# An LSTM with a rank-8 adapter: the adapter's weight generator read in 1 MB transfers of outer dimension 8

## The chip, the cores and the metric

The kernel runs on one core of a Trainium2 chip. Its metric is the device time of one execution in microseconds: 602.32 as the median of three runs before the change (600.86 to 602.75). One further execution was profiled; all rows below are from it.

## What is computed

`x` is 16 sequences of 256 tokens with 256 features, float32. First an LSTM runs over the tokens and its output is added to `x`. Then an adapter works on the result: a two-layer network of `cond` generates, for each of the 16 sequences, four weight quarters of rank 8, which act beside two shared 256 x 256 matrices.

```python
xz = einsum('ntd,dk->ntk', x, Wx) + b
def step(carry, xz_t):
    prev_h, prev_c = carry
    ai, af, ao, ag = split(xz_t + prev_h @ Wh, 4, axis=1)
    next_c = sigmoid(af) * prev_c + sigmoid(ai) * tanh(ag)
    next_h = sigmoid(ao) * tanh(next_c)
    return (next_h, next_c), next_h
x = x + lstm(x)

c = layernorm(cond) * gamma + beta
h = gelu(c @ W1 + bias1)                  # 16 x 256
w = h @ W2 + bias2                        # W2 is 256 x 8192, 8 MB
a1, b1, a2, b2 = split(w, 4), each (16, 256, 8)
u   = einsum('btd,bdr->btr', x, a2)
mid = gelu(x @ base_down + einsum('btr,blr->btl', u, b2))
v   = einsum('blr,btl->btr', b1, mid)
out = x + mid @ base_up.T + einsum('bkr,btr->btk', a1, v)
```

## The kernel before

The 256 tokens are 256 dependent steps, in 32 blocks of 8. All instructions are written out; the five engines run their own lists and meet at semaphores.

One step, on the critical path: TensorE multiplies the last hidden state with `Wh` into two banks `z` and one `z_o` (L712; 64 and 32 records of small matmuls), VectorE transposes the gates (L868, L872), ScalarE takes tanh (L422, L428, L434), VectorE forms the cell and the new `h_t` (L878 to L893). The banks are seeded beforehand by ScalarE with the projected input of the step (L358, L362).

Everything else of a block is laid into the steps. In step s of block k, TensorE transposes the `x` of block k+3 (L483), projects block k+2 with `wx` in eight pieces (L502, table `PIECES`), and does the adapter of block k-1 (L515 to L558). VectorE evacuates the projection into `proj` (L802). Then SP copies `proj` into `seed`, four transfers of 16 partitions each (L255), because the steps want it in another layout; ScalarE waits for this in step 7 of the block before, in front of that step's own second tanh (L439).

The weights of the adapter are made in the first blocks. In block 0 TensorE transposes the normed `cond` (step 2), multiplies it with `W1` (step 3, L607) and ScalarE makes `hid` from it. From step 11 on (`W_FIRST`) each step takes one of 16 portions of W2 (L633): four quarters of four portions, so the quarters begin in steps 11, 15, 19 and 23, counted from 0. Three SBUF tiles hold the quarters; the fourth goes into the first's tile.

SP issues all loads from one list, in order. A W2 portion is read in two transfers of 256 KB, 64 partitions each (L282). Each waits until the transfer three before it has landed (`UNDER_WAY`), so at most three are in flight. Between them SP issues the other loads of the block: `x` (L244), four of `w_bias` (L289, 16 partitions each) and the seeds. A wait of SP holds up all that stands behind it in the list.

Of the kernel before, what the change touches and what calls it, by code (L numbers as in the profile page):

```python
# [21 lines left out]
ACT = mybir.ActivationFunctionType  # L22
# [4 lines left out]
P = 128  # L27
NQ, NM, C = 4, 2, 32
# [11 lines left out]
LN_EPS = 1e-5  # L40
QUARTERS = (2, 1, 3, 0)
W_FIRST = 11
UNDER_WAY = 3
W_COLS = D * RANK // NQ
W_HALF = W_COLS // 2

# [3 lines left out]

N_PIECES = 8
PIECES = ((0, 0, 0, 2, 2, 4, 5, 7, 8), (0, 1, 2, 3, 4, 5, 6, 7, 8), (0, 1, 2, 3, 4, 5, 6, 7, 8))
EVACUATE_AT = (1, 3, 5, 7)
N_X = 4
WARM_UP = 6
# [2 lines left out]
def lstm_adapter(nc, x, cond, Wx, Wh, b, base_up, base_down, gamma, beta, W1, bias1, W2, bias2, out):  # L59
    ctx = ExitStack()  # L60
    with ctx:
# [6 lines left out]
        def sem(name):  # L68
# [26 lines left out]
        c_norm = sb("c_norm", [B, D])  # L95
        c_stat = sb("c_stat", [B, 5])
        c_t = sb("c_t", [P, 2, B])
        w1 = sb("w1", [P, 2, D])
        b1_col = sb("b1_col", [P, 2])
        hid = sb("hid", [P, 2, B])  # L100
        w2_tiles = [sb(f"w2_{n}", [P, 2, D * RANK]) for n in range(3)]
# [44 lines left out]
        zeroed = sem("zeroed")  # L146
        w_loaded = {n: sem(f"{n}_loaded") for n in
                    ("wx_g", "wx_if", "wx_o", "wh_g", "wh_if", "wh_o", "b", "down", "up", "ln", "cond", "w1")}
        w2_loaded = [[[sem(f"w2_loaded{q}_{i}_{r}") for r in range(2)] for i in range(NQ)] for q in range(4)]
        w_bias_zeroed, w_bias_loaded = sem("w_bias_zeroed"), sem("w_bias_loaded")  # L150
        w_placed = [sem(f"w_placed{q}") for q in range(4)]
        wx_ready, wh_ready = sem("wx_ready"), sem("wh_ready")
# [85 lines left out]
        @block.sync  # L238
        def _(sp):
            def load_x(f):  # L240
                first = f.k * TB
                if f.at_least(2):
                    sp.wait_ge(xt_psum, f.k - 1)
                sp.dma_start(x_nat[f.par][:, :], x[:, first:first + TB, :]).then_inc(x_loaded[f.par], 16)  # L244

            def load_seed(f):
                consumed = f.k * TB - TB
                if f.at_least(2):
                    for gone in (*seeded, seeded_o):
                        sp.wait_ge(gone, consumed)  # L250
                else:
                    sp.wait_ge(seeds_zeroed, f.k + 1)
                for j in range(NQ):
                    sp.wait_ge(xz_ready, f.k * XQ + (j + 1))
                    sp.dma_start(seed[f.par][32 * j:32 * j + B, :, :], proj[f.par][:, ZW * j:ZW * (j + 1)])\  # L255
                      .then_inc(seed_loaded[f.par], 16)

            def store_y(a):
                first = a.blk.k * TB
                sp.wait_ge(y_copied[a.lane], a.seq.k + 1)  # L260
                sp.dma_start(out[:, first:first + TB, :], y_nat[a.lane][a.seq.par][:, :])\
                  .then_inc(stored[a.lane][a.seq.par], 16)

            by_half = "(m p) n -> p m n"

            def load_cols(dst, src, lo, src_lo, n, name):
                sp.dma_start(dst[:, :, lo:lo + n], src.rearrange(by_half, m=NM)[:, :, src_lo:src_lo + n])\
                  .then_inc(w_loaded[name], 16)

            w2_parts = W2.rearrange("(k p) (q j h n) -> q h k p j n", p=P, q=4, j=NQ, n=W_HALF)  # L270

            def load_w2(piece):

                n, i = divmod(piece, NQ)
                q, (h, kc) = QUARTERS[n], divmod(i, 2)
                if piece == 3 * NQ:
                    sp.wait_ge(w_psum, 2)
                for r, rows in enumerate((slice(0, P // 2), slice(P // 2, P))):
                    back, half = divmod(2 * piece + r - UNDER_WAY, 2)
                    if back >= 0:  # L280
                        sp.wait_ge(w2_loaded[QUARTERS[back // NQ]][back % NQ][half], 16)
                    sp.dma_start(w2[q][rows, kc, :].rearrange("p (j h n) -> p h j n", j=NQ, n=W_HALF)[:, h],  # L282
                                 w2_parts[q, h, kc, rows]).then_inc(w2_loaded[q][i][r], 16)

            bias_q = bias2.rearrange("(q j n) -> j q n", q=4, j=NQ)

            def load_w_bias(j):
                sp.wait_ge(w_bias_zeroed, 1)
                sp.dma_start(w_bias[32 * j:32 * j + B, :, :], bias_q[j].partition_broadcast(B)).then_inc(w_bias_loaded, 16)  # L289

            load_x(Blk(0, 0))
            load_cols(wx, Wx, 2 * H, 3 * H, H, "wx_g")
            load_cols(wx, Wx, 0, 0, 2 * H, "wx_if")
            load_cols(wx, Wx, 3 * H, 2 * H, H, "wx_o")
            load_cols(wh, Wh, 2 * H, 3 * H, H, "wh_g")
            load_cols(wh, Wh, 0, 0, 2 * H, "wh_if")
            load_cols(wh, Wh, 3 * H, 2 * H, H, "wh_o")
            load_x(Blk(0, 1))
            sp.dma_start(c_gamma[:, :], gamma.partition_broadcast(B)).then_inc(w_loaded["ln"], 16)
            sp.dma_start(c_beta[:, :], beta.partition_broadcast(B)).then_inc(w_loaded["ln"], 16)  # L300
            load_seed(Blk(0, 0))
            load_x(Blk(0, 0, 2))
            sp.dma_start(w1[:, :, :], W1.rearrange("(k p) n -> p k n", p=P)).then_inc(w_loaded["w1"], 16)
            sp.dma_start(b1_col[:, :], bias1.rearrange("(k p) -> p k", p=P),
                         allow_slow_non_contiguous=True).then_inc(w_loaded["w1"], 16)
            load_cols(up_raw, base_up, 0, 0, D, "up")
            load_seed(Blk(0, 1))
            load_cols(down, base_down, 0, 0, D, "down")

            def one_block(k, front):  # L310
                if not k.at_least(1):
                    load_w2(0)
                    load_w2(1)
                if k.plus(3).exists():
                    load_x(k.plus(3))
                for piece in {0: range(2, 8), 1: range(8, 13), 2: range(13, 4 * NQ)}.get(k.k, ()):
                    load_w2(piece)
                    if 2 <= piece < 2 + NQ:
                        load_w_bias(piece - 2)
                if front:  # L320
                    load_seed(k.plus(2))
                done = follower(k.plus(-1))
                if done and done.seq.exists():
                    store_y(done)
                if early(k):
                    store_y(early(k))

            schedule(one_block)
            store_y(follower(Blk(NBLK // 2 - 1, 1)))
            for m in both:  # L330
                sp.wait_ge(tail_copied[m], 1)
# [7 lines left out]
        def _(act):  # L339
# [39 lines left out]

            def make_weights(k, s):  # L380

                if k == 0 and s == 3:

                    act.wait_ge(w_loaded["w1"], 32)
                    act.wait_ge(hidden_psum, 1)
                    for i in range(2):
                        act.activation(hid[:, i, :], aux[:, i * B:(i + 1) * B], ACT.Gelu,
# [25 lines left out]
            def one_block(k, front):  # L413
                a, e, done = follower(k), early(k), follower(k.plus(-1))
                for s in range(TB):
# [31 lines left out]
                        act.wait_ge(ht_ready[1], n + 1)  # L447
                        seed_o(ahead.par, s_next)

                    if s == 1 and not k.at_least(1):  # L450
                        evacuate_x(k.plus(2))
                    if not k.at_least(EARLY + 2):
                        make_weights(k.k, s)
# [24 lines left out]
        def _(pe):  # L478
# [115 lines left out]
            def make_weights(k, s):  # L594
# [5 lines left out]
                        ins = pe.transpose(aux[:, i * B:(i + 1) * B], c_norm[:, i * P:(i + 1) * P], ident[0:B, 0:B])  # L600
                    ins.then_inc(cond_t_psum, 1)
                if k == 0 and s == 3:
                    pe.wait_ge(w_loaded["w1"], 32)
                    pe.wait_ge(cond_t_ready, 1)
                    for i in range(2):
                        for kc in range(2):
                            ins = pe.matmul(aux[:, i * B:(i + 1) * B], w1[:, kc, i * P:(i + 1) * P], c_t[:, kc, :],  # L607
                                            start=(kc == 0), stop=(kc == 1))
                    ins.then_inc(hidden_psum, 1)
                if k == 0 and s in (4, 5):  # L610
# [8 lines left out]
                if 0 <= k * TB + s - W_FIRST < 4 * NQ:  # L619
# [6 lines left out]
                        pe.wait_ge(up_ready, 2)  # L626
                    elif kc == 0:
                        pe.wait_ge(w_biased, 2 * n + h)
                    for half in w2_loaded[q][i]:
                        pe.wait_ge(half, 16)  # L630
                    for j in range(NQ):
                        first = W_COLS * j + W_HALF * h
                        ins = pe.matmul(out_bank[32 * j:32 * j + B, 0:W_HALF], hid[:, kc, :],  # L633
# [38 lines left out]
                ins.then_inc(b_psum, 1)  # L672
            project(Blk(0, 0), range(N_PIECES))
            transpose_x(Blk(0, 1), both)
            project(Blk(0, 1), range(6))

            pe.wait_ge(w_loaded["wh_if"], 16)
            pe.wait_ge(w_loaded["wh_o"], 16)
# [2 lines left out]
            def one_block(k, front):  # L681
# [3 lines left out]
                for s in range(TB):  # L685
# [65 lines left out]
                    if front:  # L751
                        if not k.at_least(1):
                            if s == 0:
                                project(Blk(0, 1), range(6, N_PIECES))
                            if s == 1:
                                transpose_x(f, both)
                        project(f, range(pieces[s], pieces[s + 1]))
                    if not k.at_least(EARLY + 2):
# [38 lines left out]
        def _(dve):  # L797
# [63 lines left out]
            for q in range(XQ - 1):  # L861
# [34 lines left out]
            def make_weights(k, s):  # L896
# [14 lines left out]
                if 0 <= u < 2 * NQ and not between:  # L911
                    n, h = divmod(u, 2)
                    dve.wait_ge(w_psum, u + 1)
                    if u == 0:
                        dve.wait_ge(w_bias_loaded, 16 * NQ)
# [13 lines left out]
            def one_block(k, front):  # L929
                a, e, f, done = follower(k), early(k), k.plus(2), follower(k.plus(-1))  # L930
                for s in range(TB):
# [25 lines left out]
                    if s == 0 and not k.at_least(1):  # L957
                        evacuate_projection(Blk(0, 1), XQ - 1)
# [94 lines left out]
```

## Time and profile before

| | |
|---|---|
| median of three runs | 602.32 us |
| profiled execution | 606.49 us, span 604.7 |
| TensorE matmul busy | 584.7 us (97%) |
| VectorE, ScalarE busy | 502.5 (83%), 384.6 us (64%) |
| mean TensorE clock granted | 0.994 of full |
| HBM read, written | 16.05, 4.19 MB |

The profile's times are microseconds from the span's start. A busy TensorE is not one at its peak: its records overlap. "Issue" is time in which an engine waited for nothing the profile shows. The chain of waits is followed back from the last instruction. The DMA share is that of 16 engines' time and can exceed 1, since packets of one engine overlap. The page's sums run over all stages; the first 100 us differ from the rest, so the rows further below go by stretch.

### The profile page before, as it was taken

To read this page: it belongs to the slowest core of one execution; us is meant where nothing else is said; L and a number is where in the kernel's file an instruction comes from. 1 tells how busy PE (TensorE), PEld (TensorE's weight loads), DVE (VectorE), ACT (ScalarE), POOL (GpSimd) and SP (SyncE) were. 2 spreads that over 40 slices of the span, in tenths; PEclk is the share of its full clock that TensorE was granted. 3 is DMA by queue.
4 is the path that set the end of the run, shared out by engine and by line. 5 is a ranking of instruction groups with operands and counts; after the bars stand their busy time and mean duration, and the time that the engine had idled before them with its cause. 6 is when DMAs were issued, how large, how long until landed. Compare 5 with 4: busy or idle time off the path is not lost.

```text
span 604.7 us, 34273 instructions
## 1 busy us (share of the span) xinstructions
PE 584.7 (97%) x14116; PEld 440.1 (73%) x14116; DVE 502.5 (83%) x2810; ACT 384.6 (64%) x2155; POOL 47.4 (8%) x91
## 2 busy tenths in 40 slices
PE   8888989999999999999999999999999999999997
PEld 7555557777777777777777777777777777777886
DVE  4667768888888888888888888888888888888874
ACT  2555546666666666666666666666666666666663
POOL 4002122000000000000000000000000000000000
PEclk9989899999999999999999999999999999999999
DMA  7999872123332212323221132332123333212201
GB/s 195 184 179 179 174 148 45 33 37 56 56 56 56 41 27 48 55 56 56 56 42 37 37 55 57 55 56 40 40 35 56 55 56 55 45 37 26 56 21 29
DMA packets 40158, 39.75 MB, mean 66 GB/s; under 512 B 4369, under 2 KB 38977, under 8 KB 40002
## 3 DMA queue, kind: packets, MB, share of 16 engines
q1 hardware_dynamic: 39456, 37.01, 33.7%
q8 instruction: 112, 1.84, 1.4%
q0 software_dynamic: 512, 0.53, 0.5%
q14 instruction: 44, 0.36, 0.3%
q10 hardware_dynamic: 34, 0.02, 0.0%
HBM read 16.05 MB, written 4.19 MB: 33 GB/s over the span
## 4 chain that ended last, share of the span: by engine, by line
PE 93%; DVE 2%; issue 2%; DMA 2%; SPq 0%; ACT 0%; DVEq 0%; ACTq 0%
PE z L712 35%; PE x_bank L502 18%; PE z_o L712 9%; PE aux L531 8%; PE out_bank L558 7%; PE aux L515 3%; PE aux L483 2%; PE out_bank L590 2%; PE aux L538 2%; PE out_bank L633 1%; DMA x_nat<-in_x 1%; DMA seed<-proj 1%; PE out_bank L579 1%; PE x_bank L579 1%; PE x_bank L531 0%
## 5 line engine op out<-in xcount | busy, mean ns | idle before, releaser
L712 PE MATMUL z<-wh,h_t 128*16 128x96 f32 x8160 | 235.5, 249 | 5.4 <-issue 3.4
L712 PEld LDWEIGHTS z<-wh,h_t 128*16 128x16 f32 x8160 | 154.2, 96 | 110.6 <-DVE h_t L893 79.8
L868 DVE STREAM_TRANSPOSE z<-z 128x96 f32<-128x96 f32 x512 | 152.4, 298 | 71.1 <-PE z L712 47.8
L422 ACT ACTIVATE gates<-z 128x48 f32<-128x48 f32 x512 | 108.1, 211 | 122.5 <-DVE z L868 122.3
L502 PE MATMUL x_bank<-wx,x_t 128*128 128x256 f32 x512 | 153.6, 387 | 0.6 <-ACT x_t L352 0.5
L358 ACT ACTIVATE z<-seed 128x96 f32<-128x96 f32 x512 | 126.9, 248 | 4.2 <-DMA seed<-proj 4.2
L712 PE MATMUL z_o<-wh,h_t 128*16 128x64 f32 x4080 | 105.6, 220 | 4.9 <-issue 4.9
L878 DVE SCALAR_TENSOR_TENSOR prod<-gates 128x32 f32<-128x32 f32 x512 | 98.2, 192 | 0.3
L712 PEld LDWEIGHTS z_o<-wh,h_t 128*16 128x16 f32 x4080 | 80.7, 97 | 5.4 <-issue 5.3
L502 PEld LDWEIGHTS x_bank<-wx,x_t 128*128 128x128 f32 x512 | 79.1, 192 | 4.2 <-ACT x_t L352 0.7
L428 ACT ACTIVATE gate_o<-z_o 128x32 f32<-128x32 f32 x256 | 50.6, 198 | 31.7 <-DVE z_o L872 6.4
L362 ACT ACTIVATE z_o<-seed 128x64 f32<-128x64 f32 x256 | 58.3, 228 | 19.3
L872 DVE STREAM_TRANSPOSE z_o<-z_o 128x64 f32<-128x64 f32 x256 | 65.7, 257 | 5.1 <-PE z_o L712 5.0
L1001 POOL TENSOR_TENSOR xp<-x_t,h_t 128x128 f32<-128x128 f32 (+1 forms) x60 | 30.3, 527 | 473.7 <-DVE h_t L893 456.6
L434 ACT ACTIVATE z_o<-z 128x16 f32<-128x16 f32 x256 | 43.0, 168 | 25.6
L802 DVE TENSOR_TENSOR proj<-x_bank,b_all 128x256 f32<-128x256 f32 x128 | 54.0, 422 | 2.4 <-PE x_bank L502 2.3
L883 DVE SCALAR_TENSOR_TENSOR z<-prod 128x16 f32<-128x16 f32 x256 | 46.7, 182 | 8.7
L888 DVE SCALAR_TENSOR_TENSOR gates<-prod 128x32 f32<-128x32 f32 x255 | 46.9, 184 | 0.0
L434 ACT ACTIVATE tanc<-tanc 128x16 f32<-128x16 f32 x256 | 45.6, 178 | 0.0
L893 DVE SCALAR_TENSOR_TENSOR h_t<-gate_o,z_o 128x16 f32<-128x16 f32 x256 | 43.7, 171 | 0.1
L893 DVE SCALAR_TENSOR_TENSOR h_t<-gate_o,tanc 128x16 f32<-128x16 f32 x256 | 43.7, 171 | 0.0
L531 PE MATMUL aux<-xp,down 128*128 128x128 f32 x232 | 43.3, 289 | 0.0
(137 smaller groups left out, 521.9 us busy)
## 6 DMA issues: line engine op xcount, KB each, us to landing
seed<-proj SPq DMA_DIRECT2D x128, 128.0 KB, 4.4
w<-in_L_cond_W SPq DMA_DIRECT2D x33, 256.0 KB, 4.8
x_nat<-in_x SPq DMA_DIRECT2D x32, 128.0 KB, 4.1
out<-y_nat SPq DMA_DIRECT2D x32, 128.0 KB, 4.1
wx<-in_L_cond_Wx SPq DMA_DIRECT2D x2, 256.0 KB, 3.9
wx<-in_L_cond_Wx SPq DMA_DIRECT2D x1, 512.0 KB, 4.8
wh<-in_L_cond_Wh SPq DMA_DIRECT2D x2, 256.0 KB, 5.7
wh<-in_L_cond_Wh SPq DMA_DIRECT2D x1, 512.0 KB, 6.0
```

The lines of the kernel that those rows point to most:

```text
L358: act.activation(z_bank[m][:, 0:GC], seed[buf][:, s, P * m:P * m + GC], ACT.Copy)\
L362: act.activation(o_bank[:, 0:OC].rearrange("p (m c) -> p m c", c=C), seed[buf][:, s, :].rearrange("p (m q) -> p m q", m=NM)[:, :, GC:P], A ...
L422: act.activation(gates[s % 2][m][:, 0:3 * B].rearrange("p (g b) -> p g b", b=B), zt[m].rearrange("p (g c) -> p g c", c=C)[:, :, 0:B], ACT. ...
L434: act.activation(tanc[m], cell[m], ACT.Tanh, scale=0.5).then_inc(tanc_ready[m], 1)
L502: ins = pe.matmul(x_bank[q % 2][:, 0:XW].rearrange("p (m g c) -> p m g c", m=NM, c=C), x_t[f.k % N_X][:, kc, :], wx[:, kc, :].rearrange("p ...
L531: ins = pe.matmul(mid_bank[a.lane][:, cols], lhs, rhs, start=(part == 0), stop=(part == 2))
L712: ins = pe.matmul(dst, h_prev[:, kc, :], rhs, start=False, stop=(kc == 1), skip_group_check=True)
L802: dve.tensor_tensor(proj[f.par][:, q * XW:(q + 1) * XW], x_bank[q % 2][:, 0:XW], b_all[:, q * XW:(q + 1) * XW], ALU.add).then_inc(xz_ready, 1)
L868: dve.transpose(zt[m], z_bank[m][:, 0:GC]).then_inc(turned[m], 1)
L872: dve.transpose(zt_o, o_bank[:, 0:OC]).then_inc(turned_o, 1)
L878: dve.scalar_tensor_tensor(prod[m][:, :], now[:, 0:2 * B], 1.0, now[:, 2 * B:4 * B], ALU.add, ALU.mult).then_inc(prod_ready[m], 1)
L893: dve.scalar_tensor_tensor(h_t[k.par][:, m, s, 0:B], gate_o[:, B * m:B * (m + 1)], 1.0, tanc[m], ALU.add, ALU.mult).then_inc(ht_ready[m], 1)
```

## The change

W2's rows are read in another order and shape. The hidden units are renumbered: partition p = 16a + b holds unit 8b + a of a half, which makes the source of a transfer an 8 x 16 x 2048 pattern that cannot be merged into 128 rows. Each transfer reads one half of one quarter, 1 MB in rows of 8 KB, for all 128 partitions. There is no wait for earlier transfers but that for the fourth quarter's tile. To fit, W1's columns are reordered by one ScalarE activation in step 2 of block 0, and `b1` is read with the same pattern in two transfers. `w_bias` is read in eight transfers of 8 partitions instead of four of 16.

On SP the first quarter and `w_bias` go ahead of the seeds of block 1, the second quarter behind the `x` of block 3, the third behind the seeds of block 2, the fourth to the start of block 2; `x` is loaded one block earlier. TensorE waits once a quarter instead of once a portion. Block 1 is projected whole ahead of the first step, the `x` of block 2 is transposed in step 0 instead of step 1, and its projection is spread over other steps of block 0.

```diff
-PIECES = ((0, 0, 0, 2, 2, 4, 5, 7, 8), (0, 1, 2, ...
+PIECES = ((0, 0, 2, 3, 3, 4, 5, 7, 8), (0, 1, 2, ...
...
-            w2_parts = W2.rearrange("(k p) (q j h n) -> q h k p j n", p=P, q=4, j=NQ, n=W_HALF)
-            def load_w2(piece):
-                n, i = divmod(piece, NQ)
-                q, (h, kc) = QUARTERS[n], divmod(i, 2)
-                if piece == 3 * NQ:
-                    sp.wait_ge(w_psum, 2)
-                for r, rows in enumerate((slice(0, P // 2), slice(P // 2, P))):
-                    back, half = divmod(2 * piece + r - UNDER_WAY, 2)
-                    if back >= 0:
-                        sp.wait_ge(w2_loaded[QUARTERS[back // NQ]][back % NQ][half], 16)
-                    sp.dma_start(w2[q][rows, kc, :].rearrange("p (j h n) -> p h j n", j=NQ, n=W_HALF)[:, h],
-                                 w2_parts[q, h, kc, rows]).then_inc(w2_loaded[q][i][r], 16)
+            w2_q = W2.rearrange("(k b a) (q n) -> q k a b n", k=2, a=8, q=4)
+            def load_w2(n):
+                for kc in range(2):
+                    sp.dma_start(w2[QUARTERS[n]][:, kc, :], w2_q[QUARTERS[n], kc]).then_inc(w2_loaded[QUARTERS[n]], 16)
...
-            def load_w_bias(j):
+            def load_w_bias():
                 sp.wait_ge(w_bias_zeroed, 1)
-                sp.dma_start(w_bias[32 * j:32 * j + B, :, :], bias_q[j].partition_broadcast(B)).then_inc(w_bias_loaded, 16)
+                for j in range(NQ):
+                    for first in (32 * j, 32 * j + B // 2):
+                        sp.dma_start(w_bias[first:first + B // 2, :, :], bias_q[j].partition_broadcast(B // 2))\
+                          .then_inc(w_bias_loaded, 16)
...
             def one_block(k, front):
                 if not k.at_least(1):
-                    load_w2(0)
+                    load_x(k.plus(3))
                     load_w2(1)
-                if k.plus(3).exists():
-                    load_x(k.plus(3))
-                for piece in {0: range(2, 8), 1: range(8, 13), 2: range(13, 4 * NQ)}.get(k.k, ()):
-                    load_w2(piece)
-                    if 2 <= piece < 2 + NQ:
-                        load_w_bias(piece - 2)
+                    load_x(k.plus(4))
+                elif k.plus(4).exists():
+                    load_x(k.plus(4))
+                if k.k == 2:
+                    sp.wait_ge(w_psum, 2)
+                    load_w2(3)
                 if front:
                     load_seed(k.plus(2))
+                if not k.at_least(1):
+                    load_w2(2)
...
+                if k == 0 and s == 2:
+                    act.wait_ge(w_loaded["w1"], 48)
+                    halves = "p k (i a b) -> p (k i) a b"
+                    act.activation(w1_turned[:, :, :].rearrange(halves, i=2, a=8),
+                                   w1[:, :, :].rearrange("p k (i b a) -> p (k i) a b", i=2, a=8), ACT.Copy)\
+                       .then_inc(w1_ready, 1)
...
-                    for half in w2_loaded[q][i]:
-                        pe.wait_ge(half, 16)
+                    if i == 0:
+                        pe.wait_ge(w2_loaded[q], 32)
...
-            project(Blk(0, 1), range(6))
+            project(Blk(0, 1), range(N_PIECES))
```

SP's list before, from the first block's seeds on; `w_0` is the tile of W2's first quarter, `w` is W1, `x4` counts transfers:

```order
L255 DMA seed<-proj 16x8x256 x4
L244 DMA x_nat<-in_x 128x1x256
L303 DMA w<-in_L_cond_W 128x2x256
L304 DMA b_col<-in_L_cond_bias 128x2x1
L267 DMA up_raw<-in_L_cond_base_up 128x2x256
L255 DMA seed<-proj 16x8x256 x4
L267 DMA down<-in_L_cond_base_down 128x2x256
L282 DMA w_0<-in_L_cond_W 64x4x256 x4
L244 DMA x_nat<-in_x 128x1x256
L282 DMA w_0<-in_L_cond_W 64x4x256 x2
L289 DMA w_bias<-in_L_cond_bias 16x4x512
```

SP's list now, over the same place:

```order
L244 DMA x_nat<-in_x 128x1x256
L255 DMA seed<-proj 16x8x256 x4
L299 DMA w<-in_L_cond_W 128x2x256
L301 DMA b_col<-in_L_cond_bias 128x1x1 x2
L267 DMA up_raw<-in_L_cond_base_up 128x2x256
L275 DMA w_0<-in_L_cond_W 128x1x2048 x2
L284 DMA w_bias<-in_L_cond_bias 8x4x512 x8
L255 DMA seed<-proj 16x8x256 x4
L267 DMA down<-in_L_cond_base_down 128x2x256
L244 DMA x_nat<-in_x 128x1x256
L275 DMA w_1<-in_L_cond_W 128x1x2048 x2
```

The seeds of block 1 moved behind the whole first quarter and `w_bias`; the `x` of block 2 moved ahead of the first seeds.

TensorE's list before, from the projection of block 1 to step 2 (each `z` row with its `z_o` row is half of a step's records):

```order
L502 MATMUL x_bank<-wx,x_t 128x256 x6
L712 MATMUL z<-wh,h_first 16x96 x16
L712 MATMUL z_o<-wh,h_first 16x64 x8
L502 MATMUL x_bank<-wx,x_t 128x256 x2
L712 MATMUL z<-wh,h_t 16x96 x16
L712 MATMUL z_o<-wh,h_t 16x64 x8
L483 MATMUL aux<-ident,x_nat 128x128 x2
```

And now:

```order
L509 MATMUL x_bank<-wx,x_t 128x256 x8
L719 MATMUL z<-wh,h_first 16x96 x16
L719 MATMUL z_o<-wh,h_first 16x64 x8
L490 MATMUL aux<-ident,x_nat 128x128 x2
L719 MATMUL z<-wh,h_t 16x96 x16
L719 MATMUL z_o<-wh,h_t 16x64 x8
L509 MATMUL x_bank<-wx,x_t 128x256 x2
```

Two projection pieces moved ahead of step 0, and the transposition of an `x` from step 1 to step 0.

## Rows read from the trace of the kernel before

**Rows 1.** The chain, 0 to 130 us: start us, length us, what.
```profile
17.23 0.89 PE z L712 x32
...
29.11 0.86 issue
...
35.10 2.38 issue
38.76 1.48 PE z L712 x32
...
58.94 2.52 issue
...
78.62 2.53 issue
...
83.40 0.66 PE z L712 x32
...
95.72 0.90 PE z L712 x32
...
102.32 0.90 PE z L712 x32
```

**Rows 2.** VectorE, h_t lines: stretch, length, busy us (count), clock, DMA.
```profile
120.00:560.00 440.00, 67.98 (x399) 1.00 0.28 48
```

**Rows 3.** The page, groups: count | busy us, mean ns | idle, releaser.
```profile
L712 PE MATMUL z<-wh,h_t 128*16 128x96 f32 x8160 | 235.5, 249 | 5.4 <-issue 3.4
...
L712 PE MATMUL z_o<-wh,h_t 128*16 128x64 f32 x4080 | 105.6, 220 | 4.9 <-issue 4.9
```

**Rows 4.** Stretches: length, busy us by engine, clock, DMA share, GB/s.
```profile
34.00:38.00 4.00, 1.61 (x51) 1.15 (x51) 1.41 (x7) 0.99 (x6) 0.00 (x0) 1.00 1.08 183
38.00:42.00 4.00, 3.94 (x62) 2.58 (x65) 2.92 (x18) 2.51 (x14) 1.01 (x2) 0.58 0.84 164
58.00:62.00 4.00, 1.48 (x54) 1.16 (x43) 1.01 (x6) 0.75 (x4) 1.64 (x4) 1.00 0.74 166
62.00:66.00 4.00, 4.00 (x64) 2.49 (x66) 3.05 (x18) 2.02 (x13) 0.00 (x0) 0.57 0.77 183
```

**Rows 5.** The page's DMA queues: packets, MB, share of 16 engines.
```profile
q8 instruction: 112, 1.84, 1.4%
...
q10 hardware_dynamic: 34, 0.02, 0.0%
```

**Rows 6.** Stretches chosen for DMA rates, columns as in rows 4.
```profile
7.50:8.00 0.50, 0.50 (x5) 0.50 (x4) 0.50 (x1) 0.00 (x0) 0.00 (x0) 1.00 1.07 410
...
14.00:16.00 2.00, 1.84 (x8) 0.96 (x6) 1.17 (x5) 0.00 (x0) 0.56 (x1) 1.00 1.16 110
...
75.00:78.00 3.00, 3.00 (x69) 1.60 (x68) 2.73 (x17) 2.01 (x13) 0.00 (x0) 1.00 1.11 228
...
150.00:300.00 150.00, 149.15 (x3710) 112.36 (x3709) 131.02 (x742) 100.84 (x571) 9.12 (x18) 1.00 0.29 50
```

**Rows 7.** SP's queue in order of time: start us, length us, what.
```profile
13.13 0.60 SPq L244 DMA_DIRECT2D x_nat<-in_x  x1
...
14.91 0.47 SPq L267 DMA_DIRECT2D up_raw<-in_L_cond_base_up  x1
```

**Rows 8.** DMA issues: KB each, median us from issue to landing.
```profile
up_raw<-in_L_cond_base_up SPq DMA_DIRECT2D x1, 256.0 KB, 4.1
```

**Rows 9.** SP's own waits, 0 to 110 us: us in total, times, longest.
```profile
SPq L282 <- DMA w<-in_L_cond_W: 24.9, 17, 4.5
```

**Rows 10.** TensorE's waits, 0 to 110 us, columns as in rows 9.
```profile
PE z L712 <- ACT z L358: 1.3, 1, 1.3
...
PE aux L483 <- DMA x_nat<-in_x: 0.4, 1, 0.4
```

**Rows 11.** TensorE in order of time, 17 to 28 us.
```profile
18.23 1.13 PE L502 MATMUL x_bank<-wx,x_t 128*128 128x256 f32 x4
```

**Rows 12.** ScalarE in order of time, 4 to 6 us.
```profile
4.68 0.62 ACT L399 ACTIVATE wx<-wx 128x512 f32<-128x512 f32 x1
```

More of the change, by code:

```diff
@@ L42 @@
 W_FIRST = 11
-UNDER_WAY = 3
 W_COLS = D * RANK // NQ
@@ L52 @@
 N_PIECES = 8
-PIECES = ((0, 0, 0, 2, 2, 4, 5, 7, 8), (0, 1, 2, 3, 4, 5, 6, 7, 8), (0, 1, 2, 3, 4, 5, 6, 7, 8))
+PIECES = ((0, 0, 2, 3, 3, 4, 5, 7, 8), (0, 1, 2, 3, 4, 5, 6, 7, 8), (0, 1, 2, 3, 4, 5, 6, 7, 8))
 EVACUATE_AT = (1, 3, 5, 7)
@@ L97, in lstm_adapter @@
         c_t = sb("c_t", [P, 2, B])
-        w1 = sb("w1", [P, 2, D])
+        w1, w1_turned = sb("w1", [P, 2, D]), sb("w1_turned", [P, 2, D])
         b1_col = sb("b1_col", [P, 2])
@@ L148, in lstm_adapter @@
                     ("wx_g", "wx_if", "wx_o", "wh_g", "wh_if", "wh_o", "b", "down", "up", "ln", "cond", "w1")}
-        w2_loaded = [[[sem(f"w2_loaded{q}_{i}_{r}") for r in range(2)] for i in range(NQ)] for q in range(4)]
+        w1_ready = sem("w1_ready")
+        w2_loaded = [sem(f"w2_loaded{q}") for q in range(4)]
         w_bias_zeroed, w_bias_loaded = sem("w_bias_zeroed"), sem("w_bias_loaded")
@@ L300, in _ @@
             sp.dma_start(c_beta[:, :], beta.partition_broadcast(B)).then_inc(w_loaded["ln"], 16)
+            load_x(Blk(0, 0, 2))
             load_seed(Blk(0, 0))
-            load_x(Blk(0, 0, 2))
             sp.dma_start(w1[:, :, :], W1.rearrange("(k p) n -> p k n", p=P)).then_inc(w_loaded["w1"], 16)
-            sp.dma_start(b1_col[:, :], bias1.rearrange("(k p) -> p k", p=P),
-                         allow_slow_non_contiguous=True).then_inc(w_loaded["w1"], 16)
+            for kc in range(2):
+                sp.dma_start(b1_col[:, kc:kc + 1], bias1.rearrange("(k b a) -> k a b", k=2, a=8)[kc],
+                             allow_slow_non_contiguous=True).then_inc(w_loaded["w1"], 16)
             load_cols(up_raw, base_up, 0, 0, D, "up")
+            load_w2(0)
+            load_w_bias()
             load_seed(Blk(0, 1))
@@ L380, in make_weights @@
             def make_weights(k, s):
+                if k == 0 and s == 2:
[4 more added lines that the diff above has]
+                       .then_inc(w1_ready, 1)
                 if k == 0 and s == 3:
-                    act.wait_ge(w_loaded["w1"], 32)
+                    act.wait_ge(w_loaded["w1"], 48)
                     act.wait_ge(hidden_psum, 1)
@@ L448, in one_block @@
                         seed_o(ahead.par, s_next)
-                    if s == 1 and not k.at_least(1):
+                    if s == 0 and not k.at_least(1):
                         evacuate_x(k.plus(2))
@@ L602, in make_weights @@
                 if k == 0 and s == 3:
-                    pe.wait_ge(w_loaded["w1"], 32)
+                    pe.wait_ge(w1_ready, 1)
                     pe.wait_ge(cond_t_ready, 1)
@@ L606, in make_weights @@
                         for kc in range(2):
-                            ins = pe.matmul(aux[:, i * B:(i + 1) * B], w1[:, kc, i * P:(i + 1) * P], c_t[:, kc, :],
+                            ins = pe.matmul(aux[:, i * B:(i + 1) * B], w1_turned[:, kc, i * P:(i + 1) * P], c_t[:, kc, :],
                                             start=(kc == 0), stop=(kc == 1))
@@ L753, in one_block @@
                             if s == 0:
-                                project(Blk(0, 1), range(6, N_PIECES))
-                            if s == 1:
                                 transpose_x(f, both)
@@ L859, in _ @@
             dve.tensor_scalar(c_stat[:, 3:4], c_stat[:, 2:3], 1.0 / D, LN_EPS, ALU.mult, ALU.add).then_inc(ln_step, 1)
-            for q in range(XQ - 1):
+            for q in range(XQ):
                 evacuate_projection(Blk(0, 1), q)
@@ L914, in make_weights @@
                     if u == 0:
-                        dve.wait_ge(w_bias_loaded, 16 * NQ)
+                        dve.wait_ge(w_bias_loaded, 2 * 16 * NQ)
                     if h == 0 and n >= 2:
@@ L956, in one_block @@
                         add_residual(done)
-                    if s == 0 and not k.at_least(1):
-                        evacuate_projection(Blk(0, 1), XQ - 1)
                     if front and k.at_least(1) and s in EVACUATE_AT:
```

## The prediction

> **What bounds the kernel now.** I first asked where the span is spent. After the start-up the 256 recurrence steps follow one another, and the chain shows when a step's first matmul group begins [rows 1]: step 0 at 17.23 us, step 32 at 102.32. For the pace of an undisturbed step, count the h_t writes of one line, one per step [rows 2]: 399 for the two halves in 440 us, so 2.2 us a step. The first 32 steps took 102.32 - 17.23 = 85.1 us where 32 x 2.2 = 70.4 would do: 14.7 us are lost there, and nowhere else does a stretch of this size lose anything. The change only acts in this stretch.
>
> Next, what TensorE waited for. The page's groups of its recurrence matmuls put 3.4 + 4.9 = 8.3 us of the whole span down to "issue", that is, nothing the profile can name [rows 3]. Four places in the chain carry all of it, none after 81 us [rows 1]: 0.86 us at 29.11, 2.38 at 35.10, 2.52 at 58.94, 2.53 at 78.62, each in the middle of a group of equal matmuls. After a long one TensorE is slow: granted clock 0.58 of full in 38 to 42 us and 0.57 in 62 to 66, a mix of 2.4 and 1.2 GHz, after stretches in which PE was busy 1.61 and 1.48 of 4 us [rows 4]. There a group of 32 z matmuls takes 1.48 us instead of some 0.9 [rows 1].
>
> Why does the engine lack instructions? The page has a queue of instruction packets beside the data queue: 112 packets, 1.84 MB, one every 5.4 us [rows 5]. In the stretches of two of these stalls the DMA engines are busy for 1.08 and 0.74 of their time, against 0.29 later, when nothing stalls [rows 4, 6]. I read the stalls as instruction packets that came late behind data. This is an inference: no row gives a packet its engine.
>
> **The change part by part.**
>
> *W2 in eight transfers of 1 MB.* Does an outer dimension of 8 mean 8 DMA engines? The page's queue 10 holds only the two loads from ScalarE, 16 rows and 1 row, and counts 34 packets [rows 5]: 16 + 1 of data and 16 + 1 of completion fits, so a load uses as many engines as its outer dimension has, up to 16. Then W2 and w_bias fill eight engines, and the other eight carry only their halves of seeds, x and stores. If the instruction packets run on one of those, the 8.3 us of stalls go, and with them the slow clock: all that is above 2.2 us, but for about 1.3 us in steps 24 to 28, where W2 matmuls and the adapter stand in one step (z groups at 83.40 and 95.72, 12.3 us for five steps [rows 1]). The Trainium skill states the same count and adds a place, "DMA: Bandwidth & Descriptors", section on why a DMA adds 16 to its semaphore: a load from SP or ACT takes the lowest-numbered engines that divide both outer dimensions. No run here shows the numbers of the engines.
>
> The price is that eight engines hold a queue in order, and what TensorE needs stands behind W2. Rates: with all 16 engines, whole rows into all partitions moved at 410 GB/s, so eight do 205 [rows 6]. The chained pieces, 64 partitions each, moved at 228 with full engines, 114 for eight [rows 6]. Seeds, which go to 16 partitions a transfer, moved at 110, so 55 for eight [rows 6]. A quarter of W2 (2.10 MB) takes 10.2, 18.4 or 38 us by these; I take 205, the row whose target is nearest, 128 partitions. w_bias (0.52 MB, now 8 partitions a transfer) takes 2.6 to 9.5 us, the low half of a seed round (0.26 MB) 1.3 to 4.8. The seed row is nearest in form but had twice as many engines asking, so I take the middle, 6.0 and 3.0.
>
> Now the queue of the eight. up_raw was issued at 14.91 and landed 4.1 us later [rows 7, 8]; x moves ahead of it, so I let W2 begin at 18.0.
> - Quarter 0 ends at 28.2, w_bias at 34.2, seeds of block 1 at 37.2, down and x of block 3 at 38.1. ScalarE wants the seeds in step 7, which at the steady pace begins at 17.23 + 7 x 2.2 = 32.6, about 1.1 us in: it waits 37.2 - 33.7 = 3.5 us. Behind that instruction stand the step's other tanh and seed activations, on which VectorE and TensorE wait. With 1.0 us for the slow clock afterwards, step 9 begins at 37.0 + 3.5 + 1.0 = 41.5.
> - Quarter 1 ends at 48.3 (wanted in step 15, 54.7), x and seeds at 51.6, quarter 2 at 61.8 (step 19, 63.5), x and seeds at 65.1, quarter 3 at 75.6. Step 23 begins at 72.3 and reaches its W2 matmuls 1.5 us later: TensorE waits 1.8 us.
> - Step 24 begins at 72.3 + 2.2 + 1.8 = 76.3, step 32 at 76.3 + 17.6 + 1.3 + 0.7 (clock) = 95.9. Before: 102.32. Gain 6.4 us.
>
> With both unknowns at their low ends nothing waits and step 32 begins at 87.6 + 1.3 + 0.5 = 89.4: gain 12.9. With both at the high ends step 7 waits 8.8 us, TensorE in step 23 another 5.4, step 32 begins at 104.8: a loss of 2.5.
>
> *No chain.* SP waited 24.9 us in 17 waits for W2 pieces [rows 9]. These go; x and seeds are issued sooner by them, but arrive by the queue above.
>
> *x loads earlier.* x of block 2 was issued at 13.13 [rows 7], behind the first seeds; now it goes ahead of them, while SP waits for the projection, so its transposition can move to step 0. TensorE waited 0.4 us once for an x [rows 10]; that is the most this can give, and the steady pace in the sum holds it already.
>
> *Projection evened out.* Two of the eight pieces of block 1 move from step 0 ahead of it, where TensorE idles 1.3 us until the seeds [rows 10]; the two pieces took 1.13 us in step 0 [rows 11]. Cost nothing; if that cover were gone, 1.1 us. The other moved pieces change step, not number.
>
> *W1 turned.* One more activation, 128 x 512: 0.62 us, as for wx [rows 12]. It stands at the end of step 2, behind the last seeding; the next tanh waits for two transpositions by VectorE, and that gap hides some or all of it: 0 to 0.62 us, once. I take 0. The extra b1 transfer is one more issue on SP ahead of W2, inside the 18.0.
>
> Sum: -6.4 us on an execution of 606.49 (span 604.7). The median of the runs is 602.32; the same difference gives 602.32 - 6.4 = 595.9, forecast 596, with 589.4 and 604.8 for the ends.
>
> **The rivals.**
>
> *The eight engines share paths into SBUF (slower).* Price: each quarter 18.4 us instead of 10.2. Quarter 3 ends at 75.6 + 4 x 8.2 = 108.4, TensorE stands in step 23, step 32 begins near 128.2: +25.9, 628. It decides from 11.8 us a quarter (178 GB/s) on, where the gain is used up. For it: transfers into part of the partitions moved at 228 and 110 with the engines full [rows 6]. Against it: 410 into all partitions, and here all 128 are targets. The 110 GB/s of the seeds agree with such sharing.
>
> *The instruction packets run on the eight (slower).* Then a packet waits behind up to a whole 1 MB transfer, 131 KB an engine, 5.1 us at 205 GB/s, where three chained pieces put 49 KB, 3.4 us at 228. Some 11 packets fall between 18 and 76 us; each late by 1.7 us more, and about 1 us that some had been late already, is 30 us: 596 + 30 = 626. For it: nothing in the profile tells the engine. Against it: nothing either.
>
> *The new waits eat the gain (no change).* w_bias and the seeds near the seeds' own rate: 600.5 to 604.
>
> *Nothing waits (faster).* 589.4, the low end of the forecast.
>
> **How the numbers follow.** Less than 0.3% is what this kernel's measurements cannot tell from no change: 1.8 us. Forecast with its low end 0.48; gain eaten 0.12; shared paths 0.22; packets on the eight 0.18. So faster 0.48, same 0.12, slower 0.40. The forecast's own range is 589 to 600.5. The range, 589 to 614, adds the no-change case and the half of the shared-path case in which sharing is partial (quarters of up to 14 us).
>
> **What would show it.** The four "issue" places of TensorE gone, with clock 1.00 in 38 to 42 and 62 to 66; instead a wait of ScalarE for seeds in step 7 of some 3.5 us and one of TensorE for W2 in step 23; step 32 near 96. GB/s near 205 between 18 and 28 us with a DMA share near 0.5 confirms eight engines and the rate; a GB/s near 110 there, or "issue" of over 10 us, makes the prediction wrong. So would a share near 1, which says that W2 is on all 16.

## The result, and the profile after

The changed kernel is slower: 620.09 us in the profiled execution against 606.49 before, and 1.029 times the time before [1.024, 1.034], where brackets hold a 95% interval. The median of all four of its runs is 625.21, but two of them, 630.24 and 639.83, lie over 1.5% above the fastest and count in no comparison.

The chain of waits of the changed kernel (start us, length us, what), to hold against [rows 1]:

```profile
17.00 0.89 PE z L719 x32
...
24.04 4.62 SPq L255
...
28.70 4.14 SPq L255
...
33.66 14.73 DMA x_nat<-in_x
...
50.04 1.41 PE z L719 x32
...
68.52 0.66 PE z L719 x32
...
70.78 24.14 DMA w<-in_L_cond_W
...
95.67 0.66 PE z L719 x32
...
115.67 0.90 PE z L719 x32
```

These z groups open steps 0, 8, 16, 24 and 32. Eight steps at 2.2 us are 17.6; here they took 33.0, 18.5, 27.2 and 20.0. So 15.4 us are lost by step 8, where the kernel before had lost 3.9 (38.76 - 17.23 - 17.6 [rows 1]), and 12.8 after it, against 10.8 before. Step 32 begins 13.35 us later than before, which is the 13.6 us of the two profiled executions. Between those groups the chain leaves TensorE: it runs over seed issues of SP, an x that took 14.73 us to land, and the second half of the last W2 quarter, which took 24.14.

TensorE's waits, then ScalarE's (total us, times, longest), of the changed kernel:

```profile
PE aux L490 <- DMA x_nat<-in_x: 6.8, 1, 6.8
PE x_bank L509 <- issue: 4.7, 1, 4.7
PE aux L652 <- DMA w_tmp<-w_nat: 3.4, 1, 3.4
PE out_bank L640 <- DMA w<-in_L_cond_W: 2.2, 1, 2.2
...
PE z L719 <- issue: 1.4, 2, 0.9
```

```profile
ACT z L359 <- DMA seed<-proj: 9.8, 2, 5.6
```

Of the 9.8 us for seeds 4.2 belong to the start, as in the kernel before; 5.6 are new, in step 7. In the same step TensorE waits 6.8 us for the x of block 3. The two waits run side by side and the one for x ends last (48.53 us against 47.15), so the chain goes by x. "Issue" is 6.1 us instead of 8.3 [rows 3], 4.7 of it in step 2: the stalls have not gone. The w_tmp wait is a small transfer by which GpSimd places the generated weights; it had no part in the forecast.

SP's queue in order of time (start us, length us, what, how many), against [rows 7]:

```profile
15.47 1.27 SPq L275 DMA_DIRECT2D w<-in_L_cond_W  x2
16.78 3.64 SPq L284 DMA_DIRECT2D w_bias<-in_L_cond_bias  x8
20.52 12.32 SPq L255 DMA_DIRECT2D seed<-proj  x4
...
33.66 2.70 SPq L244 DMA_DIRECT2D x_nat<-in_x  x1
36.41 2.89 SPq L275 DMA_DIRECT2D w<-in_L_cond_W  x2
...
40.95 10.13 SPq L255 DMA_DIRECT2D seed<-proj  x4
51.13 3.08 SPq L275 DMA_DIRECT2D w<-in_L_cond_W  x2
```

SP's wait for VectorE in front of seed issues, whole execution, then the issue of the same x in the kernel before:

```profile
SPq L255 <- DVE proj L807: 24.1, 31, 7.1
```

```profile
26.90 0.62 SPq L244 DMA_DIRECT2D x_nat<-in_x  x1
```

The rows of the queue hold SP's waits too. Of the 12.32 us 2.2 are a wait for VectorE's `proj`, and of the 10.13 us 7.1, the longest such wait: the second group waits for the projection. But in the first group issuing itself is no longer cheap. Ten transfers went out in 5 us, and then two single seed issues took 4.62 and 4.14 us (the chain above) where one issue takes 0.6 [rows 7]. The x behind them went out at 33.66, 6.8 us later than before.

Stretches of the changed kernel (length, busy us by engine, clock, DMA share, GB/s), and the landing times of a stretch of the DMA view, 30 to 43 us (KB each, us from issue to landing):

```profile
18.00:22.00 4.00, 3.36 (x93) 2.32 (x90) 3.66 (x22) 2.95 (x17) 0.00 (x0) 1.00 0.54 132
22.00:24.00 2.00, 0.47 (x28) 0.48 (x19) 1.94 (x11) 1.41 (x9) 0.00 (x0) 1.00 0.89 129
24.00:29.00 5.00, 1.79 (x20) 1.10 (x23) 0.22 (x2) 0.99 (x1) 0.00 (x0) 0.56 0.44 149
62.00:67.00 5.00, 5.00 (x156) 3.16 (x148) 4.73 (x24) 2.74 (x17) 0.00 (x0) 1.00 0.52 211
84.00:88.00 4.00, 4.00 (x103) 2.30 (x106) 3.74 (x22) 2.53 (x16) 0.00 (x0) 1.00 0.46 191
...
30.00:40.00 10.00, 9.36 (x180) 7.54 (x169) 6.14 (x37) 5.68 (x32) 0.00 (x0) 0.76 0.65 137
...
60.00:80.00 20.00, 16.29 (x414) 9.80 (x408) 15.14 (x77) 10.31 (x58) 5.34 (x10) 0.98 0.73 165
```

```profile
seed<-proj SPq DMA_DIRECT2D x4, 128.0 KB, 14.6
```

A share near 0.5 agrees with eight busy engines. In two short stretches of later quarters all transfers together move at 211 and 191 GB/s, near the rate foreseen; while the first quarter moves they make 129 to 149, and over 30 to 40 and 60 to 80 us 137 and 165. Seeds landed 14.6 us after their issue. In 22 to 24 us TensorE was busy for 0.47 of 2 us; in 24 to 29 us the clock is 0.56 of full, between its levels of 1.2 and 2.4 GHz.

### The profile page after: what moved, and what is told of

Same layout as the page of the kernel before. It is cut to its first block, busy times and chain, and to the rows that moved or that the text cites. A ratio compares the mean times of both kernels' runs of the same rounds, so it can differ in the third digit from the quotient of the medians.

```text
span 618.3 us, 34241 instructions
## 1 busy us (share of the span) xinstructions
PE 589.0 (95%) x14116; PEld 443.3 (72%) x14116; DVE 503.2 (81%) x2810; ACT 385.5 (62%) x2156; POOL 47.3 (8%) x91
## 4 chain that ended last, share of the span: by engine, by line
PE 88%; DMA 7%; DVE 2%; SPq 2%; issue 1%; ACT 0%; DVEq 0%; ACTq 0%
PE z L719 34%; PE x_bank L509 17%; PE z_o L719 9%; PE aux L538 8%; PE out_bank L565 7%; DMA w<-in_L_cond_W 4%; PE aux L522 3%; PE aux L490 2%; DMA x_nat<-in_x 2%; PE out_bank L597 2%; PE aux L545 2%; SPq L255 1%; PE out_bank L640 1%; DMA seed<-proj 1%; PE out_bank L586 1%
```

## The experiments

Medians of the kernel before, measured beside each run, are 602.8 to 604.2. Each ratio is to them. ScalarE's seed wait always holds the 4 us or so of the start. The waits of a run are those of one profiled execution.

**The other parts alone.** The kernel before with the earlier x, the evened projection and `PIECES` of the change, W2 and `w_bias` as they were.

> The kernel before with only the other parts of the change: x loaded a block earlier, block 1 projected whole ahead of step 0, x of block 2 transposed in step 0, the new table for block 0. W2 and w_bias chained as before, W1 as it was. All theories: these parts cost or give little, within 0.5 us of 602.5 in what they do themselves. If an instruction packet falls differently, one of the four idles of 2.4 us may go or come: 599 to 606. If they alone lost over 8 us, the cause would lie here and not in W2.

603.73, ratio 1.000 [0.997, 1.003]. These parts cost and give nothing in the total, though the waits inside are others: issue is 2.9 us instead of 8.3, and ScalarE waits 3.9 us for late seeds (none before). The loss lies in how W2 and `w_bias` are read, with what belongs to it (W1's turning, `b1`).

**Seeds first**, in the changed kernel:

```diff
+            load_seed(Blk(0, 1))
+            load_x(Blk(0, 0, 3))
             load_w2(0)
             load_w_bias()
-            load_seed(Blk(0, 1))
```

> The changed kernel, with the seeds of block 1 and the x of block 3 issued ahead of the first quarter of W2 and w_bias; nothing else moves. Theory 'queue order' (what TensorE needs stands behind W2 and w_bias in the eight engines' queues): the waits of steps 7 and 8, 8.0 us over the steady pace in the changed kernel, fall under 1 us, and the time from 620 to about 612. Theory 'instruction packets' (they run on the eight and wait behind W2): steps 7 and 8 gain as well, but idle places called issue stay, some 5 us or more in steps 2 to 6, and the time stays above 608. Theory 'shared paths': W2 is as slow as it was, under 150 GB/s in the first quarter, and the gain is under 4 us.

628.1, ratio 1.039 [1.033, 1.046]: no gain over the change, against the theory. SP's queue, TensorE's and ScalarE's waits of this run:

```profile
27.10 11.54 SPq L275 DMA_DIRECT2D w<-in_L_cond_W  x2
...
47.05 11.59 SPq L275 DMA_DIRECT2D w<-in_L_cond_W  x2
...
63.04 11.88 SPq L255 DMA_DIRECT2D seed<-proj  x4
```

```profile
PE out_bank L640 <- DMA w<-in_L_cond_W: 8.5, 1, 8.5
```

```profile
ACT z L359 <- DMA seed<-proj: 13.2, 2, 9.1
```

SP now stood at W2's issues for as long (of the 11.88 us for seeds, 9.4 are a wait for VectorE). The seeds of step 7 came in time; the waits moved to seeds (9.1 us) and x (5.8) in step 15 and to W2 in step 23. Issue kept 7.2 us, in steps 7 and 10, much as the theory of instruction packets had it.

**Sixteen engines.** Outer dimension 16 in W2's, `b1`'s and W1's patterns (`a=8` becomes `a=16`), rows of 8 KB still.

> The changed kernel with an outer dimension of 16 instead of 8 for W2, W1's columns and b1; order, 1 MB transfers, no chain and w_bias as they are. Theory 'queue order': W2 moves on all engines near twice as fast, a quarter in 5 to 7 us, seeds and x wait less: steps 7 and 8 lose under 5 us instead of 8.0, step 23 nothing; 605 to 612. Theory 'instruction packets': packets of instructions still wait behind rows of 8 KB, since their engine carries W2 either way, so issue idles of some us stay: not under 605. Theory that eight engines keep instructions clear of W2: this one is slower than 620, by stalls at more packets.

625.56, ratio 1.035 [1.028, 1.041]. TensorE's waits:

```profile
PE z L719 <- issue: 14.1, 3, 5.9
PE x_bank L509 <- issue: 4.5, 1, 4.5
...
PE z_o L719 <- issue: 2.1, 1, 2.1
```

All waits for x, W2 and late seeds are gone, and "issue" is 20.7 us instead of 6.1. With SP's list as in the change, four seed issues took 2.71 us: SP no longer stood still. Much the same total hides another cause.

**Rows of 2 KB on eight engines.** Four transfers of 256 KB in place of one of 1 MB:

```diff
-                    sp.dma_start(w2[QUARTERS[n]][:, kc, :], w2_q[QUARTERS[n], kc])...
+                    for j in range(NQ):
+                        cols = slice(W_COLS * j, W_COLS * (j + 1))
+                        sp.dma_start(w2[QUARTERS[n]][:, kc, cols], w2_q[QUARTERS[n], kc][:, :, cols])...
```

> The changed kernel with each 1 MB transfer cut into four of 256 KB, so the rows are 2 KB instead of 8 KB; still an outer dimension of 8, unchained, same order. Theory 'instruction packets wait for a group of rows of the transfer under way': a group is four times shorter, the waits of instruction packets fall from 3 to 8 us to about 1 to 2, the idle of 4.7 us in step 2 goes mostly, some 5 us gained there; the waits for seeds and x stay: 612 to 616. Theory 'queue order' alone: no gain, 619 to 622, or a loss by SP's six more issues a quarter.

620.5, ratio 1.024 [1.017, 1.032]: as the change. The 4.7 us of issue in step 2 are gone, but 4.7 come elsewhere (at 75.57 us) and issue is 5.8 us in all, against 6.1. TensorE waits 8.9 us for an x and ScalarE 12.1 for seeds.

**Both together**: outer dimension 16 and rows of 2 KB.

> The changed kernel with both earlier edits together: outer dimension 16, and W2 in four 256 KB transfers of 2 KB rows per half quarter. Theory 'two costs that hide each other': rows of 8 KB hold up the instruction packets (issue 20.7 us with 16 engines, 5.8 us left with 2 KB rows), and eight engines hold up seeds, x and W2 (some 13 us with 2 KB rows, gone with 16 engines). Each edit alone let the other cost grow, so both together should go: step 32 some 14 us sooner than with 2 KB rows alone, about 97, and a time of 595 to 603. Rival 'the packet waits behind the bytes that are queued, whatever the rows': issue stays near 20 us, 618 to 626. Rival 'the costs add and each edit took all that it can': 620 - (625 - 625) = 620.

619.23, ratio 1.026 [1.022, 1.030]. My theory fell: the costs do not go together. TensorE's waits:

```profile
PE z_o L722 <- issue: 9.8, 1, 9.8
PE z L722 <- issue: 5.2, 3, 2.8
```

15.0 us of issue with small rows and all engines, and beside the stall of 9.8 in step 7 ScalarE waits 8.3 us for seeds. What all these forms still shared was that nothing held W2 back.

**w_bias behind the seeds of block 1**, on eight engines and on sixteen, both with rows of 2 KB.

> 2 KB rows on eight engines as before, but w_bias is issued behind the seeds of block 1 and the x of block 3 instead of ahead of them. Theory 'w_bias is what the seeds wait for' (0.52 MB that moved for some 10 us): the 7.9 + 2.0 us of steps 7 and 8 shrink to 0 to 2, time 610 to 614. Rival 'the seeds wait for W2's first quarter and the queue as such': steps 7 and 8 keep 7 to 10 us, 618 to 622. Rival 'the wait only moves on': seeds come in time in step 7, but those of block 2 are late in step 15 by as much, 618 to 622.

> Outer dimension 16, 2 KB rows, and w_bias behind the seeds of block 1. Theory: as outer dimension 16 with 2 KB rows, and if seeds still waited there in step 7, less by that wait: 593 to 600. Rival 'with 16 engines w_bias is no longer in the way': the same as without this edit, within 0.5%.

621.16 and 614.52, ratios 1.029 [1.026, 1.032] and 1.020 [1.016, 1.025]. On eight engines the seed wait of step 7 went as expected, and TensorE then waited 12.7 us for W2 and 5.4 for issue: the wait moves on, as in the third case, though to W2 and not to the seeds of block 2. On sixteen the intervals with and without the edit overlap, and issue is 16.2 us.

**The kernel before without its chain.** One number:

```diff
-UNDER_WAY = 3
+UNDER_WAY = 64
```

> The kernel before with UNDER_WAY 64 instead of 3: no W2 piece waits for another, rows and engines as they were. Theory 'a packet waits for a bounded number of rows, not for the whole queue': the issue stalls stay about what they were (8 us), time 600 to 606. Rival 'the packet stands behind all that is queued': six pieces are 3 MB, 13.8 us at 228 GB/s, so stalls of up to 10 us each and a time over 620. Rival 'the chain itself was the cost' (SP's 24.9 us of waits): seeds and x come sooner and W2 with them, 594 to 599.

619.12, ratio 1.023 [1.018, 1.029]. TensorE's waits:

```profile
PE z L712 <- issue: 11.5, 4, 5.3
PE z_o L712 <- issue: 4.8, 1, 4.8
```

This isolates one cause: taking only the chain away costs 16.3 us, with no other row, engine or order changed. Issue goes from 8.3 [rows 3] to 16.3 us (the two figures of 16.3 are equal by chance), so the stalls themselves are half of the loss; the other half isn't split up here. A stretch behind one of them shows the slow clock:

```profile
40.00:45.00 5.00, 5.00 (x73) 3.31 (x67) 3.10 (x18) 2.50 (x14) 1.00 (x2) 0.50 1.10 192
```

TensorE waits for no x and ScalarE for no late seeds in this run. On sixteen engines the end of the chain is paid in stalls; the late x of the change came with the eight engines.

**A chain of two** in the kernel before (`UNDER_WAY = 2`).

> The kernel before with UNDER_WAY 2 instead of 3, nothing else. Theory 'what is in flight holds up the packets': 32 KB an engine instead of 48, the issue stalls (8.3 us) shrink to 0 to 4 us, and W2 comes slower, 256 KB each 2 us or so, which step 23 may feel by 0 to 4 us: 596 to 602. Rival 'the chain is then too slow for W2': TensorE waits for W2 in steps 15 to 27 by more than the stalls return, 605 to 612. Rival 'the stalls come from seeds and x, not from W2': no change, 602 to 603.

613.97, ratio 1.015 [1.011, 1.020]. The stalls were as the theory had it: no group of "issue" of over 0.5 us is left. But SP's wait for W2, 24.9 us with three [rows 9], became 38.4, and what stands behind it is late. SP's wait and its queue, then TensorE's and ScalarE's waits:

```profile
SPq L282 <- DMA w<-in_L_cond_W: 38.4, 24, 5.1
```

```profile
58.30 20.25 SPq L282 DMA_DIRECT2D w<-in_L_cond_W  x10
```

```profile
PE aux L483 <- DMA x_nat<-in_x: 11.3, 2, 7.7
```

```profile
ACT z L358 <- DMA seed<-proj: 14.0, 3, 7.1
```

So the chain of three in the kernel before stood between two losses: more in flight stops TensorE's instructions, less stops SP's list.

**The chain in the changed form**, rows of 2 KB, on eight and on sixteen engines, and a chain of two with late `w_bias`:

```diff
+                        back, piece = divmod(2 * NQ * n + NQ * kc + j - UNDER_WAY, 2 * NQ)
+                        if back >= 0:
+                            sp.wait_ge(w2_loaded[QUARTERS[back]][piece], 16)
```

> The changed kernel in 256 KB transfers of 2 KB rows on eight engines, with the old chain put back: each W2 transfer waits until the one three before it has landed; the order of SP's list is that of the change. Theory 'the missing chain is the cause' (the kernel before without its chain alone took 619.1): little is queued ahead of an instruction packet or of a seed transfer, so the issue stalls return to 8 us or less and the seed waits to 0 to 4 us; time 600 to 608, though eight engines stay. Rival 'eight engines are a cost of their own': three transfers are 98 KB an engine, 3.8 us at 205 GB/s, W2 and the seeds stay late; 612 to 621. Rival 'the order of the list is the cost' (w_bias and a quarter of W2 ahead of the seeds): the wait of step 7 stays at 8 to 10 us with the stalls gone, 609 to 613.

> Outer dimension 16, 2 KB rows into all 128 partitions, chain of three, the change's order. Theory 'the missing chain is the cause': 48 KB an engine in flight, 1.9 us at 410 GB/s, so packets wait less than in the kernel before (stalls 0 to 4 us), W2 arrives sooner than there; seeds of block 1 stand behind a quarter and w_bias in SP's list and may be 0 to 4 us late: 595 to 604. Rival 'eight or sixteen engines is all that matters in the chained form too': same as with eight engines chained, within 0.5%. Rival 'unchained or not, w_bias and the order cost it': 610 to 617.

> Outer dimension 16, 2 KB rows, w_bias behind the seeds of block 1, and a chain of two. Theory: the least in flight (32 KB an engine), so the fewest stalls (0 to 2 us), and seeds wait least: 591 to 599, under the kernel before. Rival 'a chain of two is too slow for W2': waits of TensorE for W2 in steps 15 to 23, 600 to 608. Rival 'stalls do not come from W2 in flight': stalls of some 8 us stay and the time is that of the chain of three.

631.28, 611.27 and 624.08; ratios 1.045 [1.041, 1.049], 1.011 [1.007, 1.015] and 1.033 [1.028, 1.039]. With a chain, eight engines cost 20 us more than sixteen; without one they had cost nothing visible (620.5 and 619.2). TensorE's largest wait with eight, and ScalarE's with sixteen:

```profile
PE out_bank L648 <- DMA w<-in_L_cond_W: 18.3, 2, 11.4
```

```profile
ACT z L366 <- DMA seed<-proj: 13.9, 2, 9.7
```

So the chain put back on eight engines doesn't mend the change: it is slower by 11 us than without. With eight the supply of W2 is too slow, as with a chain of two. With sixteen step 7 still loses most: seeds stand behind a quarter and `w_bias` and keep ScalarE waiting 9.7 us, and beside that TensorE stalls for 6.4 us and waits 4.2 for x.

**Sixteen engines, chained, seeds ahead.** The seeds of block 1 and the x of block 3 before W2's first quarter, the seeds of block 2 between the halves of the second; chains of three and four.

> As e11 (outer dimension 16, 2 KB rows, chain of three), but the seeds of block 1 and the x of block 3 go ahead of W2's first quarter and w_bias, and the seeds of block 2 between the halves of the second quarter. Theory 'the rest is the order of the list': the 9.7 + 2.4 us of steps 7 and 8 fall to 0 to 3 us and little comes in their place, 597 to 603, at or below the kernel before. Rival 'the transfers themselves': the waits move to other steps, as they did when the same order was tried on the unchained form (628), 608 to 615.

> As e13 with four transfers in flight instead of three. Theory 'bytes in flight hold up the instruction packets': 64 KB an engine instead of 48, issue stalls grow by 2 to 6 us, 600 to 608. Rival 'the supply of W2 and the waits of SP set the time': 1 to 4 us less than e13.

610.94 and 607.40, ratios 1.013 [1.010, 1.015] and 1.007 [1.005, 1.009]. The late seeds are gone in both. In their place, TensorE's largest wait with three and with four in flight:

```profile
PE out_bank L649 <- DMA w<-in_L_cond_W: 10.2, 3, 6.1
```

```profile
PE z L728 <- issue: 6.9, 2, 6.6
```

For the chain of three the rival was right (the waits move). For four both came out: issue grows from 2.5 us to 8.2, as the theory had it, and the time falls by 3.5 us, as the rival had it, since W2 is no longer late. It is the same pair of limits again.

**Four, three, three, four.** Four in flight for the first and last quarter, three for the others, and TensorE waits by halves of a quarter; beside it four throughout with the same waits.

> As e13, but four transfers in flight for the first and the fourth quarter and three for the others, and TensorE waits for the second half of a quarter one step later than for the first. Theory 'there is room between the two limits': the 7.2 us of step 12 stay away (three in flight there), the 7.4 us of step 24 shrink to 0 to 3 us: 599 to 605, at or below the kernel before. Rival 'one limit takes what the other gives': a stall of 5 us or more appears in some other step, 605 to 611.

> As e14 (four in flight throughout) with TensorE's wait by halves of a quarter, which bears on a wait that e14's profile did not show. Both theories: the same time as e14 within 0.5%, 604 to 610, with one or two late instruction packets of 5 to 9 us.

606.47 and 606.09, ratios 1.003 [0.999, 1.006] and 1.004 [1.001, 1.007]. The profiled execution of the first has no wait of TensorE over 2.5 us and a span of 601.4, but its runs spread from 601.85 to 610.10. Its time lies in the rival's range, though a stall of 5 us, the rival's sign, isn't in the profile. It can't be told from the kernel before; the second is 0.4% above it. No run here beat it.

## Why the prediction was wrong

- **Step that failed: "No chain. SP waited 24.9 us in 17 waits for W2 pieces. These go".** I priced the chain's end at nothing and let x and seeds be "issued sooner by them". SP's waits for W2 went, but issuing itself stood still (4.62 and 4.14 us for two seed transfers), so the x of block 3 left at 33.66 instead of 26.90. The chain's removal alone costs 16.3 us in the kernel before. My reading is that the chain kept the DMA engines short of work ahead of instructions, seeds and x; the runs fit it, and no row shows the queues themselves. It isn't the whole cause in the changed kernel: chained on eight engines it took 631.28, and only sixteen engines, a chain and another order together (with TensorE's waits by halves) came back to 606.
- **"all that is above 2.2 us" goes with the stalls: failed.** That hung on the condition that the packets run on the idle eight. TensorE still stood 4.7 us for "issue" up to 27.20, though in 24 to 29 us the DMA share was 0.44. Part of the idea held: in the same form issue is 6.1 us with eight engines and 20.7 with sixteen. That the stalls are late packets fits the runs on sixteen engines: issue is at most 0.3 us with two transfers in flight, 2.5 to 8.5 with three, 8.2 and 8.6 with four and 15.0 to 20.7 with no limit. The spread at three says that the number in flight isn't all. No row gives a packet its engine, so neither that nor where the packets run is shown.
- **Eight engines: right, by the share** (0.54 in 18 to 22 us). **205 GB/s: reached in places only**, 211 in 62 to 67 us. The sum let it hold from 18.0 us on; the first quarter, beside `w_bias` and seeds, had 129 to 149, and 30 to 40 and 60 to 80 us had 137 and 165 with all transfers counted. There the rival of shared paths was partly right, as a rate; no run shows the paths.
- **The wait of step 7: right in place, too small, and not the one that decides.** 5.6 us instead of 3.5, inside the bound of 8.8; the 6.8 us for x beside it end later and were not in the sum, since x was let land at 38.1 and not 48.4 (33.66 + 14.73).
- **Step 23's wait for W2: 2.2 instead of 1.8.** The size is luck: the quarter landed at 94.9 us and not at 75.6, and the step was late by nearly as much. The 3.4 us for the generated weights' placement came ahead of it; no run isolates them.
- **The other parts at nothing: right** for x and the projection, 1.000. The activation that turns W1 took 1.10 us instead of 0.62 [rows 12]; it ran inside the stall of step 2, and no run isolates it.
- **The rivals.** By time the one with packets on the eight (626) came nearest, but its price was not what was lost: issue was 6.1 us in all, and the larger part lay with x, seeds, W2 and the placement. I weighed each as a property of eight engines. Without a chain eight and sixteen cost the same total by different waits: mostly x, seeds and W2 on eight, mostly stalls on sixteen. No rival weighed that.

## What to carry to other kernels

A limit on transfers in flight can be a throttle that protects whatever else uses the same DMA engines; before removing it, list everything that shares them, the instruction packets too, and test that edit by itself. When several repairs each leave the total where it was, look for what they have in common, and compare the waits and not only the totals. A row of an issue queue can hold a wait: take it off before calling the issue slow. In a queue that is issued in order, the depth of a chain is a size to be measured on both sides, since too little in flight is paid by what stands behind it.

## What the runs showed of the hardware

- An issue on SP is not always 0.6 us: with ten W2 and `w_bias` transfers before them, two single seed issues took 4.62 and 4.14 us. With the same list on sixteen engines four took 2.71 together.
- A seed transfer of 128 KB, 4.4 us from issue to landing as the median of the whole execution, took 14.6 us in the backlog (the median of four).
- Row size did not decide: on sixteen engines without a chain, issue was 15.0 us with rows of 2 KB and 20.7 with rows of 8 KB, but the longest single stall was 9.8 us with the small rows and 5.9 with the large. The Trainium skill, "DMA: Bandwidth & Descriptors", section on queues, rings and completion order, says that an engine takes its queues in turn and switches after a packet of some 9 to 17 descriptors. By that rule alone smaller rows would shorten the wait and the length of the queue would not matter; the kernel before with chains of two, three and 64 (issue of 0.3, 8.3 and 16.3 us) does not agree.
- The Trainium skill, "Runtime: NRT & Kernel Launch", section on instruction fetch, says that crossing into the next block of instructions is mostly hidden. If "issue" is late instructions, the chain of two agrees (no such wait over 0.5 us), and the kernel without a chain does not (16.3 us).
